# A four-layer convolution kernel: the last layer's weight tables made beside the first layer and kept in DRAM, its edge corrections summed in PSUM

## The reference, cut to what matters

```python
x = x + L0(gn(x))   # two blocks: three dilated 5x5 convolutions over neighbouring channels, tanh
x = x + L1(gn(x))   # 3x3 convolution of a quantised input, 16 -> 16 channels
x = x + L2(gn(x))   # 17x17 box filter per channel
# L3: a 3x3 convolution in the frequency domain
X = rfftn(gn(x), axes=(-2, -1))
Yr = conv(Xr, wr) - conv(Xi, wi) + b_real
Yi = conv(Xr, wi) + conv(Xi, wr) + b_imag
x = x + irfftn(Yr + i*Yi)
```

## Time and profile before

| | us |
|---|---|
| median of 3 runs | 6017.81 |
| lowest and highest run | 6012.23 to 6017.9 |
| profiled execution, its time | 6022.05 |
| profiled execution, its span | 6019.8 |
| TensorE busy | 5098.7 (85%) |
| VectorE busy | 3981.9 (66%) |
| ScalarE busy | 2507.5 (42%) |
| GpSimd busy | 2043.1 (34%) |

### The profile page before, as it was taken

How to read it: one execution, slowest core, us unless ns; L and a number is a source line. 1 busy time by engine, 2 the same in 40 slices (tenths; PEclk the granted TensorE clock), 3 DMA queues, 4 the chain that set the end, 5 groups by cost and what they waited for, 6 DMA issues and landing times. The chain is left out here.

```text
span 6019.8 us, 175730 instructions
## 1 busy us (share of the span) xinstructions
PE 5098.7 (85%) x77091; PEld 2739.5 (46%) x77091; DVE 3981.9 (66%) x6472; ACT 2507.5 (42%) x3849; POOL 2043.1 (34%) x1694
## 2 busy tenths in 40 slices
...
DVE  3544444444424334444344899998997999999999
...
GB/s 155 223 224 245 226 232 241 220 223 248 209 196 180 175 198 179 180 199 173 197 183 179 207 210 214 212 210 207 311 312 170 192 201 201 201 203 201 201 201 166
DMA packets 451913, 1250.35 MB, mean 208 GB/s; under 512 B 54465, under 2 KB 55217, under 8 KB 432563
## 3 DMA queue, kind: packets, MB, share of 16 engines
...
## 5 line engine op out<-in xcount | busy, mean ns | idle before, releaser
L586 PE MATMUL c_p<-c_w,wc 128*32 128x512 f16 x55296 | 3044.6, 381 | 145.3 <-issue 111.1
L586 PEld LDWEIGHTS c_p<-c_w,wc 128*32 128x32 f16 x55296 | 1547.2, 97 | 1614.5 <-issue 220.9
L644 ACT ACTIVATE c_t<-c_p,cbias,cscale 128x512 f32<-128x512 f32 x512 | 398.1, 778 | 2637.7 <-PE c_p L586 2637.7
L993 POOL TENSOR_TENSOR d_x<-d_e,d_x 128x512 f32<-128x512 f32 x340 | 457.6, 1355 | 1868.0 <-ACT d_e L982 1859.6
L519 DVE TENSOR_TENSOR a_x<-c_t,a_x 128x512 f32<-128x512 f32 x256 | 175.5, 685 | 924.2 <-ACT c_t L644 921.4
L957 PE MATMUL d_pp<-d_q,wq 128*128 128x512 f16 x2040 | 493.0, 384 | 250.5 <-DVE d_q L866 250.4
L509 DVE TENSOR_SCALAR c_y<-c_t 128x512 f16<-128x512 f32 x256 | 109.3, 427 | 857.4 <-ACT c_t L644 856.6
L1642 POOL TENSOR_TENSOR f_t<-f_t 128x512 f32<-128x512 f32 (+1 forms) x260 | 447.8, 1722 | 59.5 <-DVE f_t L1386 59.5
L1517 PE MATMUL f_P<-f_z,f_wz 128*32 128x512 f16 x6144 | 430.8, 390 | 29.7
L1481 PE MATMUL f_qp<-f_hil,f_gT 128*128 128x260 f16 (+1 forms) x3120 | 402.7, 280 | 58.8 <-DVE f_qh L1372 51.7
L957 PEld LDWEIGHTS d_pp<-d_q,wq 128*128 128x128 f16 x2040 | 175.7, 98 | 567.4 <-DVE d_q L866 392.1
...
## 6 DMA issues: line engine op xcount, KB each, us to landing
c_w<-xs SPq DMA_DIRECT2D x144, 1056.0 KB, 12.1
c_w<-ys SPq DMA_DIRECT2D x144, 1056.0 KB, 11.9
...
f_z<-f_hl SPq DMA_DIRECT2D x512, 130.0 KB, 4.7
f_z<-f_qh SPq DMA_DIRECT2D x512, 130.0 KB, 3.8
a_x<-in_x SPq DMA_DIRECT2D x256, 256.0 KB, 9.5
```

The lines of the kernel that those rows point to most:

```text
L586: t = p.matmul(pg[32 * j:32 * j + 32, :], wu[:, blk, wl, var, di, :], buf[:, bk, xl * PW + PAD + dx:xl * PW + PAD + dx + NW], start=(di == ...
L644: s.activation(tt_[n % 3][:, :], pp[:, n % 4, :], ACT.Tanh, bias=cbias[:, blk:blk + 1], scale=cscale[:, blk:blk + 1]).then_inc(c_act, 1)
L993: q.tensor_tensor(xw, te[n % 3][:, :], xw, ALU.add).then_inc(d_x, 1)
```

## The change

Two things are done. First, layer 0 makes the weight tables of all 64 row groups, one beside each of the units 8 to 71, and stores each to a DRAM tensor `wtab` (128x1792 fp16, 448 KB); layer 3 no longer computes weights, but loads a table per row group into one of three buffers. Second, two of the 12 narrow matmuls' outputs of `correct` are put into the columns to which they have to be added (the operand is read with its two halves swapped), so that PSUM holds the sum, and VectorE's `edge` goes. ScalarE's two copies get narrower (6 and 2 columns in place of 8 and 8), and VectorE's `waves` gets a wait for them (`f_k`).

```diff
+    def table_of(u):
+        return u - 8 if 0 <= u - 8 < 64 else None
 # layer0, VectorE
+    def table(ht, part):
+        flat = zw[:, 0].rearrange("p j n -> p (j n)")
+        if part == 0:
+            g4 = gm[:, :, 32:96]
+            v.scalar_tensor_tensor(mw[:, 0], g4[:, 1], chs[:, 0, ht:ht + 1], g4[:, 0], ALU.mult, ALU.add).then_inc(w_f, 1)
+            v.wait_ge(w_f, 6 * ht + 1)
+            v.scalar_tensor_tensor(mw[:, 1], g4[:, 2], chs[:, 1, ht:ht + 1], mw[:, 0], ALU.mult, ALU.add).then_inc(w_f, 1)
...
+        else:
+            v.wait_ge(w_z, 4 * ht + 4)
+            v.tensor_copy(zwh[:, 0], flat).then_inc(w_f, 1)
+            v.wait_ge(w_f, 6 * ht + 5)
+            v.tensor_tensor(zwh[:, 1], flat, zwh[:, 0], ALU.subtract).then_inc(w_f, 1)
...
+        if table_of(u) is not None and g % 2 == 0:
+            table(table_of(u), g // 2)
         (total if blk else halves)(u, g)
 # layer0, GpSimd: part 0 has four tensor_tensor of 128x192, part 1 these
+        q.wait_ge(w_f, 6 * ht + 6)
+        if ht >= 2:
+            q.wait_ge(w_td[ht % 2], 16 * (ht // 2))
+        for l in range(2):
+            q.tensor_tensor(mt[:, l], over(mwh[:, l, :], [[16, 4], [0, 8], [1, 16]]),
+                            over(pt[:, 0:8], [[0, 4], [1, 8], [0, 16]]), ALU.mult).then_inc(w_t, 1)
+            q.tensor_tensor(wz[:, l], over(zwh[:, l, :], [[16, 12], [0, 2], [1, 16]]),
+                            over(mz[:, l, :], [[0, 12], [1, 2], [0, 16]]), ALU.mult).then_inc(w_t, 1)
 # layer0, SP, behind store_y(u) and ahead of load_x
+        ht = table_of(u)
+        e.wait_ge(w_t, 4 * (ht + 1))
+        e.dma_start(K.wtab[ht], wt[ht % 2][:, :]).then_inc(w_td[ht % 2], 16)
 # layer3, VectorE
-    def edge(i):
-        n, k_ = item(i)[2], kk[i % 2]
-        v.wait_ge(f_k, 2 * (i + 1))
-        v.tensor_tensor(k_[0:n, 16:18], k_[0:n, 10:12], k_[0:n, 15:13:-1], ALU.add).then_inc(f_kk, 1)
...
         for j, (dst, off, op) in enumerate(((t1[i % 2], 0, ALU.subtract), (t2[i % 2], 4, ALU.add))):
             v.wait_ge(f_pe, 3 * i + 2 + j)
+            v.wait_ge(f_k, 2 * (i + 1))
...
-    def weights(ht, s_):
...
 # layer3, TensorE, correct(i)
-            p.wait_ge(f_mt, 4 * ht + 4)
+            p.wait_ge(f_wt[ht % 3], 16 * (ht // 3 + 1))
...
-    for f, c0, c1, o0 in ((5, 257, 259, 0), (3, 256, 258, 2), (2, 258, 259, 6), (4, 259, 260, 6)):
+    for f, c0, c1, o0, swap in ((5, 257, 259, 0, 0), (3, 256, 258, 2, 0), (2, 258, 259, 2, 1), (4, 259, 260, 2, 1)):
         for l, wl in passes:
+            edge = qq[0:n, l, 1::-1, c0:c1] if swap else qq[0:n, l, :, c0:c1]
 # layer3, ScalarE
-            s.activation(k_[0:n, 0:8], kp[0:n, 0:8], ACT.Copy).then_inc(f_k, 1)
-            s.activation(k_[0:n, 8:16], kp[0:n, 0:8], ACT.Identity, scale=inv(i)).then_inc(f_k, 1)
+            s.activation(k_[0:n, 0:6], kp[0:n, 0:6], ACT.Copy).then_inc(f_k, 1)
+            s.activation(k_[0:n, 6:8], kp[0:n, 2:4], ACT.Identity, scale=inv(i)).then_inc(f_k, 1)
 # layer3, SP
+    def load_w(ht):
+        if ht >= 3:
+            e.wait_ge(f_pe, 3 * NB * (ht - 1))
+        e.dma_start(wt[ht % 3][:, :], K.wtab[ht]).then_inc(f_wt[ht % 3], 16)
...
         if 12 <= z + 8 < NI:
             load(z + 8)
+        if i >= NB and i % NB == 3 and i // NB + 1 < 64:
+            load_w(i // NB + 1)
```

More of the change, by code:

```diff
@@ L326, in layer0 @@
         c_pe, c_act, c_hi, c_lo, c_pad, c_bn, c_mm, c_ag = (sem("c_" + n) for n in ("pe", "act", "hi", "lo", "pad", "bn", "mm", "ag"))
+        w_c, w_f, w_z, w_t = (sem("w_" + n) for n in ("c", "f", "z", "t"))
+        w_td = [sem(f"w_td{i}") for i in range(2)]
         ch = Chain(a_v)
@@ L671, in mirror, with table @@
                         q.tensor_copy(hv[:, :, to], hv[:, :, fr]).then_inc(a_pad, 1)
+                def table(ht, part):
+                    c_, sn = (over(chz[:, ht, z, :], [[1, 4], [0, 48]]) for z in range(2))
+                    G0, Gc, Gs = (over(gz[:, z, :], [[0, 4], [1, 48]]) for z in range(3))
+                    if part == 0:
+                        if ht == 0:
+                            q.wait_ge(w_c, 48)
+                            q.wait_ge(w13_ld, 144)
+                            q.wait_ge(a_v, mark["gz"])
+                        else:
+                            q.wait_ge(w_f, 6 * ht)
+                        q.tensor_tensor(zw[:, 0], Gc, c_, ALU.mult).then_inc(w_z, 1)
+                        q.tensor_tensor(zw[:, 1], Gs, sn, ALU.mult).then_inc(w_z, 1)
+                        q.wait_ge(w_z, 4 * ht + 1)
+                        q.tensor_tensor(zw[:, 0], zw[:, 0], G0, ALU.add).then_inc(w_z, 1)
+                        q.wait_ge(w_z, 4 * ht + 3)
+                        q.tensor_tensor(zw[:, 0], zw[:, 0], zw[:, 1], ALU.add).then_inc(w_z, 1)
+                        return
+                    mt = wt[ht % 2][:, 0:1024].rearrange("p (l f r o) -> p l f r o", l=2, f=4, o=16)
+                    wz = wt[ht % 2][:, 1024:1792].rearrange("p (l j r o) -> p l j r o", l=2, r=2, o=16)
+                    q.wait_ge(w_f, 6 * ht + 6)
[6 more added lines that the diff above has]
+                                        over(mz[:, l, :], [[0, 12], [1, 2], [0, 16]]), ALU.mult).then_inc(w_t, 1)
                 mirror(0)
@@ L1437, in _ @@
                 mark["ready"] = ch.step(v, v.scalar_tensor_tensor(fm[:, :, :], fm[:, :, :], -1.0, fr[:, :, :], ALU.mult, ALU.mult))
-                for s_ in range(4):
-                    weights(0, s_)
                 sums(0), low(0)
@@ L1457, in _ @@
                         q_low(z - 1)
-                    for ht, s_ in segments(z):
-                        weights(ht, s_)
             @block.tensor
@@ L1607, in mix @@
                     s.wait_ge(f_pe, 3 * i + 1)
-                    s.wait_ge(f_kk, i + 1)
+                    s.wait_ge(f_k, 2 * (i + 1))
                     wait_done(s, i - 2)
@@ L1675, in _ @@
                 q.wait_ge(f_v, mark["ready"])
-                for s_ in range(8):
-                    weights(0, s_)
                 for z in range(NI + LAG + 1):
```

126 lines of the change are left out of this document (42 added, 84 removed).

## The result

The changed kernel is **slower by 1.1%**: 6087.57 us at the median of four runs (6042.9 to 6088.06) against 6015.02 for the kernel before beside it, a ratio of 1.0106 with a 95% interval of 1.0058 to 1.0153. I had forecast 5860. Every figure per item is from a profiled execution, and so isn't to be multiplied out to a median.

A forecast was written before the change was run, and what follows sets the result against it. VectorE was taken to bound layer 3 at 5.30 us an item, DMA traffic afterwards at 4.65. Gains of 166 and 2 us less 10 in layer 0 made 158: 5860 us, range 5757 to 5945 for 8 times in 10.

The forecast's parts named there:

- the last of the DMA part: Layer 3: 4.79 us of DMA engine time an item, at an overlapping share of 1.03, takes 4.65 us.
- weaker rival: Layer 3: DMA binds harder or waits add up, up to 5.07 us an item, 5967 us; over 5905 at chance 0.18.
- Price of the table, 0.34 us an item, at most 0.62: Layer 3: DMA engine time of table loads, 0.34 at layer 2's rate, 0.62 at the stacks' price.
- the price of the stacks: Layer 3: an item's 0.533 MB of stacks take 2.90 us of DMA time, 5.4 us a MB.
- VectorE 3.69, GpSimd 2.88, ScalarE 3.92 us: Layer 3 after the change: time an item left on each engine; VectorE loses 1.59 us, GpSimd 1.75.
- it does not do what it says: Layer 3: VectorE stays the bound at 5.2 us, its GpSimd waits moving to L1404 and L1367; chance 0.02.
- TensorE 4.0, SP 4.2 to 4.3: Layer 3: us an item for TensorE without its waits, and for SP issuing with the table's added DMA.
- the stronger rival: Layer 3: DMA does not bind, SP's issue does at 4.25 us an item: 5757 us; under 5800 at chance 0.2.
- Behind it in SP's queue stand a store and the second stack: Layer 3: the table's load delays them up to 0.7 us of issue and 4 x 0.34 us of transfer.
- Layer 0, 10 us: Layer 0: making and storing tables costs 10 us, 3 from late statistics and 7 at changes of image.
- The slower outcome: Layer 0 pays more than layer 3 gains, as table stores delay window loads: 6074 us at 3.5 a unit; chance 0.04.
- The wait of `waves` for f_k costs nothing: Layer 3: the copies hang on `correct`, which runs ahead of `mix`; 0.96 us an item would cover lateness.

The follow-up runs named there:

- e17: Changed kernel with each item's output store written as one contiguous block, same bytes and packets: 5859.29 us, ratio 0.9729 to before.
- e12: The changed kernel itself run once more, unaltered: 6091.41 us, ratio 1.0124 to before.
- e3: Changed kernel with layer 3 loading tables 0 to 2 only and using them for all 64 row groups: 5992.11 us, ratio 0.996.
- e1: Kernel before with only the edge sum moved into PSUM, weights still made in layer 3: 6017.51 us, ratio 1.0014.
- e13: Changed kernel with each output store cut to 16 of its 128 rows: 5769.78 us, ratio 0.9587.
- e5: Changed kernel with layer 3's lag raised from 8 to 10 items, a third f_z buffer and x loads six ahead, not eight: 6120.2 us, ratio 1.0193.
- e9: Changed kernel with lag 10, three f_z buffers and 22 f_x buffers, x loads kept eight ahead: 6121.81 us, ratio 1.0168.
- e4: Changed kernel with the table's load issued two steps earlier, behind the second stack: 6110.25 us, ratio 1.0137.
- e8: e5 with the table's load issued at the row group's second item, behind the second stack: 6056.86 us, ratio 1.0075.
- e2: Changed kernel with the edge sum put back on VectorE, so the tables alone: 6077.75 us, ratio 1.0096.
- e16: e10 with x loads six items ahead instead of eight: 5961.09 us, ratio 0.9923.
- e18: Changed kernel, lag 8, with x loads six items ahead instead of eight: 6048.79 us, ratio 1.0061.
- e10: Changed kernel with only the weights' factors (512 columns) in DRAM, spread by GpSimd in layer 3, lag 10, 22 f_x buffers: 5992.08 us, ratio 0.9948.
- e7: Changed kernel with the second stack's eight copies issued by GpSimd instead of SyncE, lag 8: 6004.12 us, ratio 0.9986.

## Why the prediction was wrong

**The step that failed** is the last of the DMA part: "The share can read above 1, since packets overlap: 1.03 over 30 us in layer 0. 4.79 / 1.03 = 4.65." It took a share from a stretch of other transfers for one that layer 3 could reach, and packet durations for fixed costs. With layer 3's own stores at their full size the share was at most 0.95 over these stretches, whatever stood in its way, and the engine time grew. In us per item: 4.79 was forecast and 5.24 measured; at 1.03 that makes 5.24 / 1.03 = 5.09, and the share of 0.95 the rest, 5.52. So of the 0.87 us 0.44 come from longer packets and 0.43 from the share. e17 changed where the stores go, and both terms came back: 4.70 / 1.01 = 4.65.

The profiled execution can be followed to its end. The forecast for it was 5864 us. From the first `waves` of a row group to the last (4653.9 to 6031.5 us, before 4667.0 to 6011.1) the items took 33.5 us longer where 166 less were forecast, and what stands ahead of them took 13.1 us less where 8 more were: 5864 + 166 + 33.5 - 8 - 13.1 = 6042, against 6042.9. In e12 the same two terms are 63.5 us longer and 13.3 us later.

That e17's 5859.29 us lies within 1 us of the forecast is luck in part: its engine time is 0.09 us an item under the forecast one and its share 0.02 under, two misses that cancel, and 4.45, from which the sum starts, was measured with the strided stores. The prediction said that durations which aren't fixed "would make me wrong most", and gave that no chance of ending slower: its weaker rival stopped at 5.07 us an item. Nor were the tables needed for it to fail: e3, with three of the 64 loads, stood at 5.32.

The packets' mean durations in ns, by size, from the trace's own records over 5000 to 5800 us (to 5700 for the two with 1/8 of the stores). Packets of 2048 bytes are x loads and output stores, of 4160 the stacks, of 3584 the table:

```
                      2048 B   4160 B   3584 B   DMA share
before                 117      303       -      0.84
before, 1/8 stores     114      281       -      0.64
after                  125      330      214     0.95
after, 1/8 stores      116      298      188     0.92
e17, contiguous        104      310      197     1.01
```

An item has 256 packets of 2048 bytes, 128 of 4160 and 32 of 3584, over 16 engines. From before to after the first two kinds add 0.13 and 0.21 us an item, and the table stands at 0.43 where 0.34 was forecast. From after to e17 the packets of 2048 bytes, half of which are the stores, give back 0.33 us of some 0.5, the stacks 0.16 and the table 0.04. The records don't tell a store's packet from a load's. With the stores nearly gone from the kernel before, the packets of 2048 bytes that are left last 114 ns for 117, so there a store's packet looks much like a load's; that it is so in the changed kernel isn't shown. From the rows of before nobody could have priced the stores apart.

**By its other steps:**
- *Price of the table, 0.34 us an item, at most 0.62.* Measured 128 x 0.214 / 16 = 1.71 us a table, 0.43 an item. Too low by 0.09, inside the bounds; part of the 0.44 above.
- *"2.90 us: 5.4 us a MB", the price of the stacks.* It gave all that was left of 4.45 to the stacks. By the records of before the packets of 2048 bytes take 256 x 117 / 16 = 1.87 us an item, not 1.55, and the stacks 128 x 303 / 16 = 2.42: 4.5 us a MB, or 220 GB/s where the prediction had 184. At that price the table's upper bound would have been 0.52, not 0.62; the forecast didn't rest on it.
- *VectorE 3.69, GpSimd 2.88, ScalarE 3.92 us.* Measured 3.53, 2.94 and 3.90. Right. But "layer 3 has none" (no room on VectorE) read waits as work. I had seen the waiting inside L1410 and kept it in the sum all the same. Removing the edge alone gave nothing (e1), because turns with GpSimd, not VectorE's own work, made the 5.30. That is the rival "it does not do what it says", its waits moving into L1404 and L1367: true of e1, and not of the changed kernel, where GpSimd's 1.75 us went too and the instructions did shrink (L1404's 1151 ns to 683, and L1367's 679 rose to 710 only).
- *TensorE 4.0, SP 4.2 to 4.3.* TensorE ran an item at 3.83 between two stalls. e13, where traffic bounds less, took 4.27 us an item, and SP waited for VectorE and TensorE in 47 of 700 us, so issued for 3.98. That 4.27 lies at the stronger rival's 4.25 doesn't show that SP bound it: the DMA share was still 0.92.
- *"Behind it in SP's queue stand a store and the second stack, ... and `correct` needs that stack four steps on."* The place is right, TensorE did come to wait there. But it is where the traffic's lateness shows, not its cause (e5, e9), and moving the table's load away made nothing faster with lag 8 (e4, 1.0137), though it gave 1% with lag 10 (e8 against e5).
- *Layer 0, 10 us; its rival.* TensorE's busy time in block 1 is 1453.81 for 1455.7, and it never waited for L404's result there. One pair of profiles doesn't give the price: layer 0's last matmul ended at 3340.1 us before and at 3326.9 after, but over the four profiled executions without tables it is 3337.6 at the mean (3334.6 to 3340.1), and 3343.3 over the thirteen with whole tables (3326.9 to 3355.7). That is some 6 us for the 10 forecast, less than the scatter. The slower outcome came true in layer 3, by no mechanism that I had listed.
- *The wait of `waves` for f_k costs nothing.* e2, without it and with `edge` back, ran at 1.0096 against the change's 1.0106 and 1.0124: within the intervals. In the changed kernel VectorE stood idle 1.2 us of 800 ahead of `waves`.
- *Not listed: the clock.* After the pause shown above TensorE works its next item at a lower clock, 1.27 us more for 24 matmuls. The granted clock in layer 3 is 0.98 before and in e13, 0.94 in e17 and 0.89 in the changed kernel, lower where TensorE waits longer; how much of the time it adds by itself wasn't tried.

**What stays open.** Why stores to rows 1 MB apart hold up the traffic, whether through their own packets, the other transfers or both. The Trainium skill ("DMA: Bandwidth & Descriptors", Latency and other measured facts) reports copies at 207 GB/s down to 103 for row pitches of 512 KB up to 8 MB (rows of 16 KB) and calls the cause, several streams in the same channels of memory, an inference. e17 agrees in direction (214 to 254 GB/s over all traffic), but tells neither pitch from order of rows nor one address bit from another. Stores whose 8 rows of a channel follow each other, at the same places in the output, weren't tried, nor was e17's store with the factors of e16. Why lag 10 made it worse (e9, 1.0168) and x loads six ahead better (e18 against e12, e16 against e10) is only described: engine-us per item of 5.39 against 5.24 and 4.99 against 5.14, and the second stack's last copy landing 13.5 us after its issue in e9 and 6.6 in e18, against 9.5 and 9.9 in the two profiles of the changed kernel. That more transfers stand in the queue at a time, and packets so get longer, is a guess. Open too is why e7, with the same bytes and packets, has an engine time of 4.75: T2, in which bytes alone count, can't have it.
